# Cross-attention and a quantised feed-forward on one core: attention output kept in head rows and moved by transfers, one value buffer, event places set anew

## The reference, cut to what matters

```python
def attention(tokens, context):
    Q, K, V = heads(tokens @ Wq), heads(context @ Wk), heads(context @ Wv)
    attn = softmax(einsum('bhnd,bhmd->bhnm', Q, K) * SCALE)      # 512 x 1601 per head
    return merge(einsum('bhnm,bhmd->bhnd', attn, V)) @ Wo + bo
def ffn(x):
    return fp4_linear(silu(fp4_linear(x, w_gate)) * fp4_linear(x, w_up), w_down)
x = x + attention(layernorm(x), ctx_768)
x = x + ffn(layernorm(x))
```

## Time and profile before

| | |
|---|---|
| median of three runs | 3528.58 us (3525.02 to 3530.06) |
| profiled execution, its own time | 3532.97 us |
| its span, first to last instruction | 3531.2 us |
| PE busy | 3420.3 us (97%), 19606 matmuls |
| DVE busy | 2947.5 us (83%) |
| ACT busy | 2298.8 us (65%) |
| POOL busy | 1036.9 us (29%) |
| mean granted clock of PE, share of full | 0.988 |
| transfers, share of 16 DMA engines | 28.6% |

### The profile page before, as it was taken

How to read it: one execution, slowest core, us unless ns; L and a number is a source line. 1 busy time by engine, 2 the same in 40 slices (tenths; PEclk the granted TensorE clock), 3 DMA queues, 4 the chain that set the end, 5 groups by cost and what they waited for, 6 DMA issues and landing times.

```text
span 3531.2 us, 55990 instructions
## 1 busy us (share of the span) xinstructions
PE 3420.3 (97%) x19606; PEld 1560.4 (44%) x19606; DVE 2947.5 (83%) x6697; ACT 2298.8 (65%) x4512; POOL 1036.9 (29%) x1114
## 2 busy tenths in 40 slices
PE   7899999999999999999999999999999999999996
PEld 3333444444444444444444444444444444444334
DVE  6878888888888988888888888988888888888865
ACT  2667666667666667666667666667666667666662
POOL 1323222333322333222333322333222333322222
PEclk7999999999999999999999999999999999999998
DMA  4332233232232332233232232332232232232210
GB/s 81 57 51 45 39 57 50 34 62 36 49 51 44 53 44 45 40 57 48 36 62 35 49 52 43 54 44 43 42 57 46 38 62 32 49 55 35 38 24 8
DMA packets 154263, 163.02 MB, mean 46 GB/s; under 512 B 58071, under 2 KB 127080, under 8 KB 153984
## 3 DMA queue, kind: packets, MB, share of 16 engines
q1 hardware_dynamic: 153984, 159.45, 28.6%
HBM read 46.22 MB, written 8.39 MB: 15 GB/s over the span
## 4 chain that ended last, share of the span: by engine, by line
PE 72%; DVE 23%; ACT 2%; POOL 1%; issue 1%; DMA 1%; SPq 1%; ACTq 0%; DVEq 0%
PE out_ps L912 18%; PE score_ps L901 16%; PE piece_ps L926 16%; DVE piece_max L1264 13%; PE work L865 6%; PE work L876 4%; PE work L840 3%; PE work L832 3%; ACT probs L1028 1%; PE work L856 1%; PE work L821 1%; DVE ctx_T L1134 1%; DVE ctx_T L1130 1%; PE work L850 1%; PE work L873 1%
## 5 line engine op out<-in xcount | busy, mean ns | idle before, releaser
L1028 ACT ACTIVATE probs<-score_ps 128x512 f32<-128x512 f32 (+1 forms) x3328 | 1884.0, 600 | 923.7 <-PE score_ps L901 916.0
L1264 DVE TENSOR_REDUCE piece_max<-piece_ps 128x1 f32<-128x400 f32 (+1 forms) x4096 | 2110.3, 566 | 360.6 <-PE piece_ps L926 347.8
L926 PE MATMUL piece_ps<-k_stack,q_stack 96*128 96x400 bf16 (+1 forms) x4096 | 1297.5, 339 | 40.2 <-DVE piece_max L1264 28.2
L901 PE MATMUL score_ps<-q_stack,k_stack 99*128 99x512 bf16 (+1 forms) x3328 | 1252.2, 385 | 19.6 <-DMA q_stack<-neg_rows 5.3
L912 PE MATMUL out_ps<-probs,v_ones 128*17 128x512 f32 x6656 | 877.1, 599 | 0.4
L926 PEld LDWEIGHTS piece_ps<-k_stack,q_stack 96*128 96x128 bf16 x4096 | 386.0, 98 | 801.9 <-DVE piece_max L1264 548.2
L901 PEld LDWEIGHTS score_ps<-q_stack,k_stack 99*128 99x128 bf16 (+1 forms) x3328 | 324.2, 99 | 641.7 <-ACT probs L1028 494.4
L1316 POOL TENSOR_TENSOR h<-h,h_grid 128x704 f32<-128x704 f32 (+1 forms) x68 | 111.8, 1644 | 888.4 <-DVE h_grid L1092 888.4
L865 PE MATMUL work<-wgu_T,xq_T 128*128 128x512 f32 (+1 forms) x1080 | 333.7, 425 | 0.5
L912 PEld LDWEIGHTS out_ps<-probs,v_ones 128*17 128x17 f32 x6656 | 110.3, 95 | 269.4 <-issue 218.4
L865 PEld LDWEIGHTS work<-wgu_T,xq_T 128*128 128x128 f32 x1080 | 198.1, 191 | 43.9 <-issue 3.8
(11 more groups left out here) (173 smaller groups left out, 2893.4 us busy)
## 6 DMA issues: line engine op xcount, KB each, us to landing
k_stack<-k_parts SPq DMA_DIRECT2D x256, 150.1 KB, 3.6
k_stack<-k_parts SPq DMA_DIRECT2D x256, 100.1 KB, 3.9
ctx_in<-in_ctx SPq DMA_DIRECT2D x47, 384.0 KB, 3.8
k_stack<-k_parts SPq DMA_DIRECT2D x256, 50.0 KB, 3.7
q_stack<-q_parts SPq DMA_DIRECT2D x256, 48.0 KB, 2.8
x_in<-in_x SPq DMA_DIRECT2D x16, 512.0 KB, 5.0
q_stack<-q_parts SPq DMA_DIRECT2D x256, 32.0 KB, 2.1
resid<-in_x SPq DMA_DIRECT2D x62, 128.0 KB, 2.6
```

What stands on the lines that cost most here:

```text
L901: pe.matmul(score_ps[0:r, n % SCORE_RING, :], k_stack[:, par, slot(g, j), m * P:m * P + r], q_stack[:, par, slot(g, j), :], start=True, st ...
L926: pe.matmul(piece_ps[:, n % PIECE_RING, 0:hi - lo], q_stack[0:SROWS, par, slot(g, j), t * P:(t + 1) * P], k_stack[0:SROWS, par, slot(g, j) ...
L1028: act.activation(probs[0:r, step % 2, j, :], score_ps[0:r, (PER_GROUP * m + j) % SCORE_RING, :], ACT.Exp, scale=SCORE_SCALE).then_inc(prob ...
L1264: dve.tensor_reduce(piece_max[:, row, c:c + 1], piece_ps[:, n % PIECE_RING, 0:piece_at[c + 1] - piece_at[c]], AX_X, ALU.max).then_inc(piec ...
```

## The change

Six things are changed. Line numbers in the order rows below are those of each kernel.

1. `heads_out` has no PE round any more. After ACT's copy, SP moves each head's 16 rows of `group_out` into `heads_T`, which now holds dimensions in rows and 512 tokens in columns, two buffers by batch (`move_heads`, four transfers). A transfer gathers the four rows of sums as 128x16 into `inv_sum`; DVE inverts them (`heads_inv`); SP writes them to a DRAM buffer (`inv_out`) and reads them back with each row spread over 16 partitions (`inv_spread`); for each pair of groups POOL multiplies 128x512 in place (`heads_norm`).
2. `heads_T` as a round is gone: PE's transposes, ACT's copy. out_proj reads the new `heads_T` and waits for POOL.
3. In the tail, group 3's sums are spread straight from `group_out` by four SP transfers, ACT's queue moves the heads, and DVE inverts and multiplies for each quarter (`heads_last`).
4. `v_ones` has one buffer. The value rounds come late in a batch (`V_AT`), the last four at the start of the next one (`v_late`); ACT's copy waits until PE is through with the old values.
5. The stack transfers behind a group's first head are issued two half steps later (`LOADS_AT`), behind `heads_out` on SP.
6. Nearly all tables are new: `POST_AT`, `TAIL_AT`, `OWN_AT`, `PRE_AT`, `STACK0_AT`, `MAX_AT`, `PIECE_WEIGHT`, `SCORE_PLACE`.

```diff
 POST_AT = [
-    [4, 6, 6, 7, 9, 11, 16, 19, 19, 20, 22, 22, 23, 26, 29, 30, 34],
...
+    [12, 12, 13, 13, 13, 16, 18, 20, 22, 22, 23, 23, 23, 29, 29, 34],
...
+V_AT = [83, 89, 102, 106, 107, 107, 108]
+LOADS_AT = 2
+INVERT_AFTER, SPREAD_AFTER, NORM_AFTER = 4, (4, 6), 8
-MAX_AT = [22, 23]
+MAX_AT = [22, 24]
-SCORE_PLACE = [0.1225, 0.3125, 0.5225, 0.7625]
+SCORE_PLACE = [0.2025, 0.3525, 0.6625, 0.7525]
...
+def move_heads(queue, of, g, heads):
+    for j in heads:
+        queue.dma_start(heads_T[head_rows(g, j), of % 2, g // 2, :], group_out[32 * j:32 * j + HEAD_DIM, :]).then_inc(heads_moved, 16)
...
+                elif name == "heads_out":            # SP
+                    sp.wait_ge(group_taken, count(of, PHASES, g + 1))
...
+                    rows = group_out[HEAD_DIM:P:32, :].rearrange("j (n c) -> j n c", c=HEAD_DIM)
+                    sp.dma_start(inv_sum[:], rows).then_inc(sums_moved, 16)
+                    move_heads(sp, of, g, range(PER_GROUP))
+                elif name == "inv_out":
+                    sp.wait_ge(inv_ready, count(of, PHASES, g + 1))
...
+                    sp.dma_start(inv_rows[g % 2].rearrange("j (n c) -> (j n) c", c=HEAD_DIM), inv_sum[:]).then_inc(inv_out, 16)
+                elif name == "inv_spread":
+                    sp.wait_ge(inv_out, 16 * count(of, PHASES, g + 1))
...
+                    rows = inv_rows[g % 2].rearrange("j (o q) -> j o q", o=1).broadcast_to([PER_GROUP, HEAD_DIM, NQ])
+                    sp.dma_start(head_inv[to, :], rows).then_inc(inv_spread, 16)
...
-                elif name == "heads_out":            # PE
-                    for t in range(QT):
-                        last = pe.transpose(work[:, t * P:(t + 1) * P], group_out[:, t * P:(t + 1) * P], ident[:])
-                elif name == "heads_T":
-                    for k in range(2):
-                        last = pe.transpose(work[:, k * P:(k + 1) * P], heads[:, old % 2, event[1], k * P:(k + 1) * P], ident[:])
+                elif name == "out_proj":
+                    pe.wait_ge(heads_normed, count(old, PHASES // 2, 2 + t if kind == "tail" else 2))
+                    for k in range(2):
+                        last = pe.matmul(work[:, 0:D], heads_T[:, old % 2, k, t * P:(t + 1) * P], wo_sb[:, k, :], start=(k == 0), stop=(k == 1))
...
+                    if kind != "start":              # ACT, v_proj and v_late
+                        act.wait_ge(pv_done, count(batch if name == "v_proj" else old, STEPS, (PHASES - 1) * KEY_TILES + m + n))
...
+                elif name == "heads_inv":            # DVE
+                    dve.wait_ge(sums_moved, count(of, 16 * PHASES, 16 * (g + 1)))
...
+                    dve.reciprocal(inv_sum[:], inv_sum[:]).then_inc(inv_ready, 1)
+                elif name == "heads_last":
...
+                    dve.reciprocal(head_inv[new_group, tokens], head_inv[new_group, tokens]).then_inc(last_inv, 1)
...
+                    dve.tensor_tensor(rows, rows, head_inv[:, tokens], ALU.mult).then_inc(heads_normed, 1)
...
+                elif name == "heads_norm":           # POOL
...
+                    pool.tensor_tensor(rows, rows, head_inv[:], ALU.mult).then_inc(heads_normed, 1)
```

162 lines of the change are left out of this document (107 added, 55 removed), and 22 rows, old and new, of tables (PIECE_WEIGHT, POST_AT, TAIL_AT).

## The result

The changed kernel takes 3565.45 us (median of 4 runs, 3562.06 to 3567.65), the kernel before in the same job 3526.89: a ratio of 1.0107, interval 1.0091 to 1.0123, 38.6 us slower. I had forecast 3506, with 3470 to 3538 as range. The profiled execution took 3567.1, its span is 3564.8, against 3531.2 before.

A forecast was written before the change was run, and what follows sets the result against it. The kernel was taken as PE-bound on average, DVE-bound in short stretches. Middle batches -29 us, first batch -1, last +2.8 and tail +5 summed to -22 to -23, giving a median of 3506 us, range 3470 to 3538.

The forecast's parts named there:

- new places: Middle batch: the new places of everything else counted at nothing, though 548 us of short waits could matter either way.
- the maxima's gate: Ends of groups: score waits 0 to 1.3 us for the maxima's transfer; net +0.8 us a batch, ends -1.2 and +5.2.
- the late spread: Out_proj at half step 12 waits for the normalised output: 0.2 us a batch, ends 0 and 4.
- PE loses the transposes: Middle batch: heads_out and heads_T rounds go from PE, counting nearly in full, 2.7 us less a batch.
- Rival C: The spread is late by 2 us in each batch: +3 us in all, 3531 us; chance 0.07.
- The landing in DRAM: Sums written to DRAM: taken to land in 1.8 us like `out`, against the skill page's rule that HBM targets are heaviest.
- Rival A: PE waits 1.3 us at each of four group ends for the transfer into `q_stack`: +39, 3568 us; chance 0.13.
- DVE -0.4: Middle batch: DVE's multiplication goes, 1.7 us less work, counted as 0.4 us by DVE's 23% of the chain.
- Rival D: The new order also removes a twentieth of the 548 us of waits for reductions: 27 us more, 3479; chance 0.20.
- First batch -1: First batch gives four of seven value rounds to the second: -1 us, ends 0 and -7.
- last +2.8: Last batch gets four value rounds without giving any: +5.5 less 2.7 for the transposes, +2.8 us.
- tail +5: Tail: spreads, inversion and product before out_proj take 6.4 us instead of 2.6; counted +5 us, ends +2 and +9.

The follow-up runs named there:

- free_delay: free_kept with only the first quarter's steps from out_proj to xq_scale moved two to six half steps later, pieces unchanged: 3561.84 us.
- free_new: Changed kernel with its tables and one value buffer, but nothing moved, inverted, spread or normalised; out_proj multiplies a constant: 3525.39 us.
- free_kept: Kernel before with its exact order, heads_out and heads_T rounds dropped from the finished sequence; out_proj reads a constant: 3505.08 us.
- e_g0: Changed kernel with the chain of sums two half steps earlier at the batch's start alone, last stack transfers and context behind its first issue: 3537.40 us.

## Why the prediction was wrong

The runs make a ledger, in us of the median: before 3527; transposes out, order kept, 3505 (-22); first quarter late by up to six half steps, 3562 (+57); changed tables and one value buffer, 3525 (-37); the transfers themselves, chain early at the batch's start, 3537 (+12); the chain late, as changed, 3565 (+28). All but the third are narrow edits. The third is all other tables, the loads' places and the value buffer together, and no run parts them.

That this third step is in the main a repair of the delay is my inference. The quarter stands at the same half steps in free_delay and in free_new. This is free_new's first group:

```profile
1132.92:1188.83 55.91, 54.25 (x317) 25.50 (x316) 47.07 (x112) 37.12 (x74) 19.45 (x25) 1.00 0.31 54
```

It is as long as free_delay's 55.4, but holds 39 more matmuls (the late value rounds stand there), its clock is 1.00, and PE is idle for 1.7 us instead of 3.2. The other three groups of this batch are together 3.4 us shorter than free_delay's (156.0 for 159.4).

By middle batch, forecast and measured (lengths on average over the 14):

| step of the sum | forecast | measured |
|---|---|---|
| transposes and DVE's multiplication go | -2.7 - 0.4 | -1.2 (free_kept less before) |
| new places, with the maxima's gate | 0 + 0.8 | +1.0 (free_new less free_kept) |
| transfers without a wait | 0 | +0.2 (e_g0 less free_new) |
| the late spread | +0.2 | +2.2 (after less e_g0) |
| sum | -2.1 | +2.2 |

Times 14 this is -29 against +30. So 59 us of the miss lie in these batches, and the whole miss is 61 (-22.6 forecast, +38.6 measured). Two steps failed, by about the same; the row of the new places is small and hides two large numbers.

- **PE loses the transposes:** that it counts "nearly in full" is the first step that failed. With DVE's share it was forecast at 3.1 us a batch and is worth 1.2, 26 us too much over 14 batches. "PE is busy 209.5 of 212" was the wrong reading: the matmuls' busy time covers small waits, and where the next operand comes from ACT or DVE, a removed step goes over in part into the next wait (free_kept's waits for ACT grew by 17 us).
- **The spread, "0.2 us of waiting a batch, with ends at 0 and 4":** this is the second step that failed, by 2.0 us a batch or 27 us; it lies within the ends but is ten times the value. The chain itself came as worked out. `inv_out` was issued 18.3 us behind the batch's first score, as computed (1156.8 for a batch at about 1138), and POOL was done at 26.3, within the computed 24.5 to 28.7. Out_proj's place, 25.0 in e_g0, was put at 24.5. The middle of my own interval was a wait of 2.1 us, and I took 0.2, because four late value rounds stand before the place; they moved it from 24.5 to 25.0. What the sum lacked altogether is the clock: four of the 14 batches lost another 1.7 us behind the wait. POOL's product takes 1.26 us and not 1.0; the row of 1034 ns mixed shapes. Rival C, at 0.07, was this mechanism; its price of 2 us a batch was right and its time was not, since it stood on the other gains.
- **"The new places of everything else I count at nothing, for want of a row":** in the net it failed by little in the middle batches, where free_new is 1.0 us longer than free_kept and the forecast had 0.8 for the maxima. That is luck: behind it stand +57 for the first quarter's move and -37 for the rest. The move was in the diff, and DVE's steps for it could have been laid beside the three banks of the ring.
- **The landing in DRAM.** I set the rule of the Trainium skill's page "DMA: Bandwidth & Descriptors" (section on the anatomy of a DMA) aside because of `out`. The changed kernel's rows fit it better:

```profile
out<-x SPq DMA_DIRECT2D x62, 128.0 KB, 1.8
...
inv_rows<-inv_sum SPq DMA_DIRECT2D x63, 8.0 KB, 3.0
```

  8 KB in pieces of 64 bytes take 1.2 us longer to land than 128 KB in rows of 1 KB, and 0.9 longer than a move within SBUF (2.1). No run tells whether the target, the pieces or what else was under way made it so: `out` itself landed in 3.6 us in the second group of the batch shown and in 1.7 in the fourth. The section cited describes transfers that GpSimd issues; here SP issues them. The nearest row was near in target and not in form.
- **The maxima's gate, +0.8:** it didn't come (3.7 us in all), though the score is now issued 2.9 to 3.7 us behind the transpose. Rival A was wrong.
- **DVE -0.4:** not to be told apart. Rival D's sign was right for the waits (548 to 430) and wrong for the time: shorter waits for one releaser are no gain when the order has others.
- **First batch -1, last +2.8, tail +5:** -3, +4.1 and +6.2. The first is within what two executions of the old order differ by (213.0 and 209.5). Out_proj comes 7.1 us behind ACT's copy, 6 to 7 were forecast; the reciprocal takes 0.95 (1.0), the product 0.29 (0.3). The rest of the tail's number is nearly right by chance: a lower clock, which the forecast didn't have, is in it.

Open: which of the many places of the changed tables costs how much, and whether some order with the complete mechanism beats before. No version here did: 3505 is what the old order takes without any way out, and 3537 the best complete one.

## What to carry to other kernels

In a kernel whose engines are in step by hand, the work that a change removes is only one part of its price; the earliest time at which its result is there is another. Find what it pushes later, and lay that block beside the buffers between the engines. Here work taken from the busiest engine was worth about half (0.45, and 0.7 when added); a run that drops it with everything else at its place, and its twin that does the work twice, cost little and should come first. When a sum gives an interval, take its middle unless there is a reason not to. And look at PE's granted clock behind each stop, in all batches and not in one: the microseconds at half speed there belong to its price.
